# Routed sweep: third groups of 64 places with both parts side by side, and an expert's last weight part split in its own piece's first two up blocks

## The reference

```python
xn = layernorm(x)
s = recurrent(xn, W1, b1, W2, b2, init_h)         # 512 -> 3 x 1024, a scan over time, 1024 -> 512
# mixture of experts, E = 32, inner width I = 1024
shared = (silu(xn @ sgw) * (xn @ suw)) @ sdw
logits = xn @ gate_w
e, v = argmax(logits), max(logits)                # one expert for each token
xs = xn * sigmoid(v)
routed = (silu(xs @ rgw[e]) * (xs @ ruw[e])) @ rdw[e]
out = x + s * silu(shared + routed)
```

## Time and profile before

| | us |
|---|---|
| three timed runs | 3884.31, 3889.35, 3890.14 (median 3889.35) |
| the profiled execution's own time | 3882.45 |
| its span, first to last instruction | 3880.8 |
| PE / PEld / DVE / ACT / POOL busy, whole span | 3813.0 / 3271.0 / 2106.0 / 2007.8 / 723.3 |
| the routed sweep, 2540 to 3881: PE / PEld / DVE / ACT / POOL busy | 1304.9 / 1219.5 / 928.2 / 713.7 / 466.9 |
| the same stretch: DMA share, GB/s | 0.69, 236 |

### The profile page before, as it was taken

The page is one execution under the profiler, slowest core; times in us unless marked ns, Lnnn a source line. Parts: engine busy times, 40 slices in busy tenths (PEclk is TensorE's granted clock), DMA queues, the critical chain, the costliest instruction groups (busy, mean ns, idle before and its releaser), DMA issues.

```text
span 3880.8 us, 57690 instructions
## 1 busy us (share of the span) xinstructions
PE 3813.0 (98%) x19358; PEld 3271.0 (84%) x19359; DVE 2106.0 (54%) x3199; ACT 2007.8 (52%) x2860; POOL 723.3 (19%) x841
## 2 busy tenths in 40 slices
PE   8999999999999999999999999989999999999998
PEld 6888888888877888888888888878999999999997
DVE  5332323333256555555555555566667767677674
ACT  3222222222237767677676767754455556565553
POOL 2011010101115100000000000022333334343333
PEclk9999999999999999999999999999999999999999
DMA  5222222222121100000110000066666768687673
GB/s 172 90 90 100 92 89 84 92 100 92 74 77 55 52 33 33 32 32 32 44 53 32 32 32 33 22 241 222 224 223 234 274 213 278 233 274 254 221 271 125
DMA packets 309383, 481.11 MB, mean 124 GB/s; under 512 B 32570, under 2 KB 208827, under 8 KB 305476
## 3 DMA queue, kind: packets, MB, share of 16 engines
q1 hardware_dynamic: 271700, 361.19, 26.9%
q0 software_dynamic: 37616, 119.08, 8.9%
HBM read 364.73 MB, written 102.99 MB: 121 GB/s over the span
## 4 chain that ended last, share of the span: by engine, by line
PE 65%; DVE 2%; issue 2%; ACT 1%; DVEq 1%; DMA 0%; ACTq 0%; SPq 0%; POOLq 0%; POOL 0%
PE bank L87 15%; PE bank L89 15%; PE bank L88 15%; PE bank L1828 11%; PE bank L1205 6%; PE bank L1209 3%; PE bank L1778 1%; DVE yo L1726 0%; DVEq L1347 0%; DVE wlo L1474 0%; DVE th L1708 0%; DVE hs L1088 0%; ACT L1055 0%; ACT w_hi L93 0%; DVE yo L1722 0%
## 5 line engine op out<-in xcount | busy, mean ns | idle before, releaser
L87 PE MATMUL bank<-txT,whi 128*128 128x256 f32 (+2 forms) x2048 | 612.5, 299 | 8.9 <-ACT tsg L1608 4.5
L89 PE MATMUL bank<-txT,wlo 128*128 128x256 f32 (+2 forms) x2048 | 608.3, 297 | 0.0
L88 PE MATMUL bank<-txT,whi 128*128 128x256 f32 (+2 forms) x2048 | 608.2, 297 | 0.0
L87 PE MATMUL bank<-xT,w_hi 128*128 128x512 f32 x1536 | 598.3, 390 | 0.0
L88 PE MATMUL bank<-xT,w_hi 128*128 128x512 f32 x1536 | 598.0, 389 | 0.0
L89 PE MATMUL bank<-xT,w_lo 128*128 128x512 f32 x1536 | 598.0, 389 | 0.0
L1474 DVE TENSOR_TENSOR wlo<-raw,whi 128x1024 fp32r<-128x1024 f32 x372 | 445.8, 1220 | 40.7 <-ACT whi L1469 40.7
L1828 PE MATMUL bank<-whi,thT 128*128 128x512 f32 x1264 | 412.4, 397 | 10.3 <-issue 10.3
L648 DVE TENSOR_TENSOR h_act<-h_act,psU 128x512 f32<-128x512 f32 x128 | 88.1, 688 | 607.4 <-PE psU L89 607.3
L1469 ACT ACTIVATE whi<-raw 128x1024 fp32r<-128x1024 f32 x372 | 384.1, 1050 | 35.8 <-DMA raw<-in_L_ffn_routed_down_w 19.7
L87 PEld LDWEIGHTS bank<-txT,whi 128*128 128x128 f32 x2048 | 389.3, 190 | 13.5 <-DVE th L1708 5.2
(11 more groups left out here) (213 smaller groups left out, 7596.4 us busy)
## 6 DMA issues: line engine op xcount, KB each, us to landing
raw<-in_L_ffn_routed_gate_w SPq DMA_DIRECT2D x124, 512.0 KB, 3.8
raw<-in_L_ffn_routed_up_w SPq DMA_DIRECT2D x124, 512.0 KB, 5.3
raw<-in_L_ffn_routed_down_w SPq DMA_DIRECT2D x124, 512.0 KB, 5.6
xT_dram<-xT SPq DMA_DIRECT2D x16, 2048.0 KB, 6.3
xT<-xT_dram SPq DMA_DIRECT2D x14, 2048.0 KB, 8.1
xs_dram<-x_in SPq DMA_DIRECT2D x16, 1024.0 KB, 4.3
ss_dram<-y_sb SPq DMA_DIRECT2D x64, 256.0 KB, 2.0
ss_dram<-ry SPq DMA_DIRECT2D x64, 256.0 KB, 2.1
```

The lines of the kernel that those rows point to most:

```text
L87: pe.matmul(out, w[0], x[0], start=start, stop=False)
L88: pe.matmul(out, w[0], x[1], start=False, stop=False)
L89: return pe.matmul(out, w[1], x[0], start=False, stop=stop)
```

## The change

It does two things in the routed sweep.

For a piece of 10 units, the 64 unused columns of the third group in h's high part get the low part of the 64 places (`remainder_beside`, a DVE subtraction for each b). The down matmuls of that group then take this one stationary operand, high places beside low places, with the high and the low weights (`packed`): 16 matmuls in place of 24. The result has the high places' sums in partitions 0 to 63 and the low places' in 64 to 127, and DVE adds them (`total_packed`). h_mul gets two more waits, since the columns must be free and the remainder taken.

Part D1 of an expert is no longer split at the end of the piece before, but in the expert's own piece, its first half behind h_hi / h_lo of block 0, its second behind those of block 1.

```diff
...
     WIDE = (GROUPS - 1) * STEP + 1
-    assert NI == 8 and PARTS == 2 * RING and NU % UNIT == 0 and NU <= D
+    assert SIZES[1] * UNIT == 2 * P + P // 2 and NI == 8 and PARTS == 2 * RING and NU % UNIT == 0 and NU <= D
     x_rows = x.rearrange("b s d -> (b s) d")
...
         yo_free = k.sem("yo_free")
+        beside = k.sem("remainder_beside")
+        half_summed = k.sem("half_summed")
...
                 with eng.If(full > 0):
-                    if first:
-                        for q in OWN:
-                            own(q)
+                    for q in OWN if first else (D1,):
+                        own(q, e, p)
                     with eng.Fori(0, MOST) as i:
                         with eng.If(full > i):
-                            piece(p + i, e, MOST_UNITS, False, None)
-                piece(p + full, e, n, split, full if first else None)
+                            piece(p + i, e, MOST_UNITS, False, False, None)
+                piece(p + full, e, n, split, first, full)
...
-        def own_part(eng, own, q, full):
+        def own_part(eng, own, q, e, p, full, halves=(0, 1)):
             with eng.If(full < 1):
-                own(q)
+                own(q, e, p, halves)
...
-            def own(q):
-                split_hi(act, q, 0)
+            def own(q, e=0, p=0, halves=(0, 1)):
+                if halves[0] == 0 and not (isinstance(e, int) and e == 0):
+                    for g in range(GROUPS):
+                        act.wait_ge(y_mm[g], p + 1)
+                split_hi(act, q, e, halves)
...
-            def piece(p, e, n, split, full):
+            def piece(p, e, n, split, first, full):
                 def silu(b):
...
                             act.wait_ge(u_mm, p * NI + 2 * q + 2)
-                        elif q == D0:
+                        else:
                             act.wait_ge(d0_mm, p * 2 + 4)
-                        else:
-                            for g in range(GROUPS):
-                                act.wait_ge(y_mm[g], p + 2)
                         split_hi(act, q, e + 1, halves)
-                first = full is not None
                 for b in range(NI):
...
                     if first and b in (0, 2, 4):
-                        own_part(act, own, OWN[b // 2], full)
+                        own_part(act, own, OWN[b // 2], e, p, full)
+                    if not first and full is not None and b < 2:
+                        own_part(act, own, D1, e, p, full, (b,))
                 if first:
...
                 third(act, n, lambda: gated(2), lambda: act.sem_inc(zs_done[2], 1))
-                hi(D1)
...
-            def own(q):
-                split_lo(dve, q, 0)
+            def own(q, e=0, p=0, halves=(0, 1)):
+                split_lo(dve, q, e, halves)
...
-            def piece(p, e, n, split, full):
-                first = full is not None
+            def piece(p, e, n, split, first, full):
                 def h_mul(b):
...
                     dve.wait_ge(u_mm, p * NI + b + 1)
+                    if b >= 1:
+                        dve.wait_ge(hlo, p * NI + b)
+                    if b >= 2:
+                        dve.wait_ge(beside, p * NI + b - 1)
                     dve.tensor_tensor(h[b % 2][:], sg[b % 2][:], psU[b % 2][:, 0:PIECE], ALU.mult).then_inc(h_done, 1)
+                def remainder_beside(b):
+                    if isinstance(n, int):
+                        return dve.sem_inc(beside, 1)
+                    few = slice(2 * P, 2 * P + P // 2)
+                    with dve.If(n > 2 * STEP):
+                        with dve.If(n < MOST_UNITS):
+                            dve.tensor_tensor(hT[:, 0, b, 2 * P + P // 2:3 * P], h[b % 2][:, few], hT[:, 0, b, few],
+                                              ALU.subtract).then_inc(beside, 1)
+                        with dve.Else():
+                            dve.sem_inc(beside, 1)
+                    with dve.Else():
+                        dve.sem_inc(beside, 1)
...
+                def total_packed():
+                    dve.wait_ge(y_mm[2], p + 2)
+                    dve.wait_ge(ss_loaded[2], (p + 1) * 16)
+                    dve.wait_ge(yo_free, p + 1)
+                    dve.tensor_tensor(yo[2][:], psY[2][:], ss[2][:, 0:D], ALU.add)\
+                        .then_inc(half_summed, 1)
+                    dve.wait_ge(half_summed, p + 1)
+                    dve.tensor_tensor(yo[2][0:P // 2], psY[2][P // 2:P], yo[2][0:P // 2], ALU.add).then_inc(z_done[2], 1)
...
                     h_mul(b)
+                    if b >= 1:
+                        remainder_beside(b - 1)
                     if b == NI - 1:
...
                     if first and b in (0, 2, 4):
-                        own_part(dve, own, OWN[b // 2], full)
+                        own_part(dve, own, OWN[b // 2], e, p, full)
+                    if not first and full is not None and b < 2:
+                        own_part(dve, own, D1, e, p, full, (b,))
                     if not first and b >= 2:
                         lo(b // 2 - 1, (b % 2,))
+                dve.wait_ge(hlo, p * NI + NI)
+                settle(dve, settled)
+                remainder_beside(NI - 1)
                 if first:
...
                 def absent():
+                    dve.sem_inc(half_summed, 1)
                     dve.sem_inc(z_done[2], 1)
...
+                def total_of(size):
+                    if size < MOST_UNITS:
+                        return total_packed()
+                    dve.sem_inc(half_summed, 1)
+                    total(2)
                 def last():
-                    total(2)
+                    if isinstance(n, int):
+                        total_of(n)
+                    else:
+                        by_size(dve, n, total_of, SIZES[1:])
                     result(2)
...
                 third(dve, n, last, absent)
-                lo(D1)
...
+            def packed(p, half):
+                q = D0 + half
+                pe.wait_ge(beside, p * NI + (half + 1) * KH)
+                for kb in range(KH):
+                    b = half * KH + kb
+                    for w in (whi, wlo):
+                        mm = pe.matmul(psY[2][:], hT[:, 0, b, 2 * P:3 * P], w[q][:, kb, :],
+                                       start=b == 0 and w is whi, stop=b == NI - 1 and w is wlo)
+                return mm
+            def down_third(p, n, half, done):
+                with pe.If(n > 2 * STEP):
+                    by_size(pe, n, lambda size: (down(half, 2) if size == MOST_UNITS else packed(p, half)).then_inc(done, 1),
+                            SIZES[1:])
+                with pe.Else():
+                    pe.sem_inc(done, 1)
...
                     pe.wait_ge(z_done[2], p + 1)
-                    third(pe, n, lambda: down(0, 2).then_inc(d0_mm, 1), lambda: pe.sem_inc(d0_mm, 1))
+                    down_third(p, n, 0, d0_mm)
                     ahead = pe.value_load(listed[0:1, 1, bass.ds(p + 1, 1)], min_val=LEAST, max_val=MOST_UNITS)
...
                         down(1, g).then_inc(y_mm[g], 1)
-                    third(pe, n, lambda: down(1, 2).then_inc(y_mm[2], 1), lambda: pe.sem_inc(y_mm[2], 1))
+                    down_third(p, n, 1, y_mm[2])
...
```

## The result

| | us |
|---|---|
| changed kernel, median of 6 runs | 3905.6 (3903.6 to 3906.3) |
| kernel before, 6 runs beside them | 3889.7 (3884.3 to 3891.7) |
| ratio, with its 95% interval | 1.0044 (1.0033 to 1.0056) |
| profiled execution of the changed kernel, its span | 3905.9, 3904.3 (before: 3882.45, 3880.8) |

Forecast were 3889 and "no change" as the likeliest; it is slower by 15.9 us between the medians, just inside the range of 3868 to 3906. A second comparison (the experiment `changed_again`) gave the same ratio, 1.0044 (1.0030 to 1.0057): 3897.9 against 3882.7. Its trace is the better one to set against the trace of before, whose execution took 3882.45, as long as the median there; in the first comparison the runs of before were some 7 us longer than their own trace.

What follows compares the result with a forecast made beforehand. TensorE was taken to bound the routed sweep, almost without waits. Terms of -22.0 + 7.3 + 9.2 + 0.8 + 4.5 gave -0.2 us, so 3889 for the median; the 8-in-10 range was 3868 to 3906.

Steps and rivals of the forecast that it cites:

- no change: Whole kernel: a measured time within about 0.2%, 7.8 us, of the kernel before; chance 0.45.
- The packing's step: Down parts of size-10 pieces: 16 matmuls for 24 save 1.82 us per piece, 21.8 us over twelve.
- the last: Last piece, a size 10 whose end DVE sets: 0.91 us gained less 0.72 for the second add, so 0.2.
- the main line of the h chain behind a size 8: Size-8 pieces after a size 8: D1's halves delay h products, 0.8 us lost per piece, 7.3 over nine.
- Behind a size 10: Size-8 pieces after a size 10: h_mul(0) at S+8.05, 2.4 us lost where 0.56 are now; five pieces, 9.2.
- D1's absence: Tail before h_mul(0): without D1, 0.7 us gained after a size 10, nothing after a size 8.
- The term for D0: End of size-8 pieces: down weights D0 may land later; 0.5 us on nine pieces, 4.5 us, between 0 and 20.
- rival (b): Tail of every size-8 piece: D0 lands late, 2.2 us on nine size-8 successors, total 3909 us; chance 0.2.
- Rival (a): Start of pieces: D1's halves hide and h_mul(0) comes earlier, before S+6, total about 3865 us; chance 0.2.
- Rival (c): DVE's longer loop: code leaves the instruction buffer, each of 31 passes pays a fetch, 80 us, total 3970; chance 0.04.
- The step that failed: Block 4 of size-8 pieces: g(4) waiting for silu(2) sets the piece's whole lateness, h-5.66, h being h_mul(0)'s time.
- the size-10 pieces: Up part of a size 10 after a size 10: g(3) late by 0.1 us, six pieces, 0.8 us.

Runs made afterwards that it cites:

- changed_again: The changed kernel without an edit, run again on one chip beside the kernel before: 3897.9 us against 3882.7, ratio 1.0044.
- packed_only: Changed kernel with only the packed third group kept, D1 split at the end of the piece before: 3875.9 us, ratio 0.9985 to the kernel before.
- remainder_alone: Kernel before plus the remainder subtraction, its branches and added waits; third group still 24 matmuls, D1 as before: 3888.2 us, ratio 1.0014.
- one_half_behind: Changed kernel with only DVE's second half of D1 in block 1, the rest split at the end of the piece before: 3867.8 us, ratio 0.9965 to before.
- act_half_first: Changed kernel with ACT's half of D1 placed ahead of h_hi instead of behind it in blocks 0 and 1: 3892.7 us, ratio 1.0032 to before.
- x_ahead_of_silu7: Changed kernel with the next piece's first x group split ahead of silu(7) and h_mul(7): 3907.4 us, ratio 1.0067 to the kernel before.
- d1_moved_only: Changed kernel with only D1's move into blocks 0 and 1; third group unpacked, no remainder or added waits: 3912.2 us, ratio 1.0080 to before.

## Why the prediction was wrong

The packing's step held to the hundredth: 1.82 us per size-10 piece, and 0.1 to 0.2 for the last. So did the main line of the h chain behind a size 8: h_mul(0) unmoved, h_mul(1) 3.35 us and h_mul(2) 6.6 behind it, stalls at blocks 3 and 4 released by silu (L1613), 0.82 us a piece where 0.8 stood (0.89 in the second trace). Behind a size 10 the mechanism was right and the size off: h_mul(0) at S+7.7, not 8.05, so 1.43 us a piece, not 1.83; the first 0.9 of it are at block 2. I had given D1's absence 0.7 us in that tail. By `packed_only` (h_mul(0) at S+8.8 with D1 there) it is 1.1.

The term for D0 (4.5 us, and rival (b)'s mechanism) did not occur. ACT's wait for the down weights fell:

```profile
ACT whi L1471 <- DMA raw<-in_L_ffn_routed_down_w: 5.8, 9, 0.9
```

It was 14.3 us in the kernel before. Near 3909 though (b)'s number came, its cause did not. Rival (a) fell with h_mul(0) at S+6.45. Rival (c) fell too. h_mul(0) is where it was and DVE's blocks take 2.75 to 2.9 us, so no pass of its loop pays 2.6 us more. The two DMA queues that the page calls instruction moved 70 packets in the whole execution, where they had moved 67; one fetch in each of 31 passes would have been 31 more. And from 2700 to 3880 us no trace of the changed kernel or of an experiment has a wait of TensorE ended by issue that is longer than 0.2 us. So nothing here shows the fetch that the Trainium skill describes ("Runtime: NRT & Kernel Launch", Instruction fetch mechanics) beyond the first jumps.

**The step that failed** is "The last decides: the piece is late by h+5.86-11.52 = h-5.66 in all", which puts what comes behind block 4 at nothing. I followed DVE's lateness to the last place at which the up part needs it and took the chain to end there. But that sentence only says by how much TensorE slips; DVE, 3.0 us late, and TensorE, 0.8 late, are still 2.2 us closer than before, and I asked nowhere who is next to need DVE. The trace had the answer: after TensorE's last matmul of `down(0, 0)` comes a transpose that needs x_lo, and x_lo stands behind h_mul(7). My own figure of 2.75 to 2.9 us for DVE's cycle against 2.88 should have told that the lateness lives on to there.

How exactly it decides, the traces show, in the size-8 piece that starts at 3387.78 in the kernel before (us after the piece's start in each):

| kernel | x_lo starts | last matmul of `down(0, 0)` | transposes start | x_lo + 0.75 |
|---|---|---|---|---|
| before | 24.45 | 25.99 | 26.22 | 25.20 |
| remainder_alone | 24.74 | 26.06 | 26.29 | 25.49 |
| one_half_behind | 25.53 | 25.99 | 26.27 | 26.28 |
| act_half_first | 26.59 | 26.11 | 27.33 | 27.34 |
| x_ahead_of_silu7 | 26.91 | 26.84 | 27.65 | 27.66 |
| d1_moved_only | 27.35 | 26.80 | 28.09 | 28.10 |
| changed_again | 27.41 | 26.87 | 28.16 | 28.16 |
| changed, first trace | 27.64 | 26.83 | 28.39 | 28.39 |

The transposes start at the later of two times: the last matmul + 0.23, and x_lo + 0.75. That holds not in this piece alone but in the 15 later size-8 pieces of all 12 traces, to 0.02 us. Before there were 26.22 - 25.20 = 1.0 us of slack (x_lo could come so much later without a wait), in each of the 15; DVE's new lag there is 3.0. The arithmetic that was missing: 3.0 - 1.0 = 2.0 us a piece in all behind a size 8, of which 0.9 is already paid in the up part, so 1.1 more at the first transposes (1.2 to 1.7 in the first trace): 15.8 us for the 15 pieces. Behind a size 10 the lag is 3.5, 1.4 of it paid, and 1.1 are left again.

The rest is lost one step behind, where TensorE needs x_lo of the second group:

```profile
3423.98 0.68 DVE L1675 TENSOR_TENSOR txT<-bank,txT 128x512 fp32r<-128x512 f32 x1
```

```profile
3424.95 0.49 PE L1889 MATMUL bank<-whi,thT 128*128 128x512 f32 x1 [0.23 <-DVE txT L1675]
```

It comes 3.42 us behind the first x_lo (3.34 before), and TensorE, released by the first, is there 0.2 us sooner (3.21 us behind the first transposes before). Where another size 8 follows, its next matmul starts 0.96 us behind this x_lo and the piece loses 0.55 us; where a larger one follows, the second transposes start 0.75 behind it and 0.24 is lost. Two pieces lose 1.2, since part 3's weights came late. Together 7.4 us, and 15.8 + 7.4 = 23.2.

Set into the sum of the prediction: -0.2, less 4.5 for D0, less 2.5 for the stalls that were smaller (14.0 for 16.5), less 0.8 for the size-10 pieces, plus 0.4 for the first three pieces, plus the missing 23.2, gives +15.6, the difference of the second trace. That the median stayed within the range is luck: a term of 23 us was missing, 7.8 us of terms that did not come stood against it, and the range's upper end was taken from rival (b), which did not occur.

The table also explains the version that won: one half in block 1 makes DVE 1.1 us late at x_lo, which is the slack. That is shown by `one_half_behind` and its repeat. That the lag and not the packing is the cause is shown by `d1_moved_only`; that it is not the later fetch, by `x_ahead_of_silu7`, where x_lo moved by 0.5 us and the transposes with it, and by ACT's waits for up weights, which account for some 1.3 of the 23.2 us.

## What to carry to other kernels

When work is put into a loop whose engine's own cycle is as long as the bottleneck's, its lateness is not used up at the first stall: follow it to the last consumer of that queue, and at each place compare it with the slack there, less what the bottleneck has already slipped. Moving one item ahead in a late queue moves the wait, not the debt. Taking a stall away brings every later meeting forward: look at what lands by DMA behind it (here part 3, which had 2.3 us of room before the change and none after it). Of work that must go somewhere, split it and put in each place only as much as the slack there: here one half of 1.1 us into 1.0 us of slack, and the kernel is 13 us faster than before instead of 16 slower.

## What was not expected of the hardware

A DVE instruction that waits for the one just ahead of it on DVE starts 0.19 us later than one that doesn't (0.67 instead of 0.48 us behind the other's start, `remainder_alone`). The branches of the remainder, which in a size-8 piece end in a semaphore increment and no subtraction, cost DVE's chain nothing that these traces show, as I had taken.

Two executions of the changed kernel, at the same granted clock of 0.993, differed by 8 us in their spans (3904.3 and 3896.4), nearly all of it in the down parts of the size-8 pieces; those of `one_half_behind` came within 1 us (3867.2 and 3866.5). It would be easy to say that a version without slack passes on what jitter the other engines have. But the kernel before, with 1.0 us of slack, differs as much between the same two comparisons (medians 3889.7 and 3882.7), so that is not shown.
